# Side test by columns, picked sums right behind the search, the 400-column first count on VectorE, and the last norm batch by batch

## What is computed

```
# attention: 16 heads, 16 memory keys in front of 512 causal ones
dots = where(causal, neg, mix_heads(q @ k.T * scale, pre_proj))
vk   = top_k(dots, 64)[0][..., -1:]          # the 64th largest score of a row
attn = softmax(where(dots < vk, neg, dots))  # only scores >= vk are kept
x    = x + (mix_heads(attn, post_proj) @ v) @ Wo + bo
# mixture of experts: a shared layer and the two best of 8 experts
scores = sigmoid(layernorm(x) @ router_w.T)
gates  = scores * one_hot(top_k(scores, 2)).sum()
x = x + shared(layernorm(x)) + sum_e(expert_e(layernorm(x)) * gates_e)
```

## Time and profile before

| | us |
|---|---|
| median of 3 runs | 1032.5 (1032.15 to 1034.19) |
| the profiled execution | 1035.09 |
| its span, first to last instruction | 1033.4 |
| mean granted clock of PE | 0.951 of full |
| PE / VectorE / ScalarE / GpSimd busy | 909.2 / 849.7 / 747.8 / 468.6 |

### The profile page before, as it was taken

One profiled execution on the slowest core, in us unless ns is written; L12 is line 12 of the kernel. 1 busy time (PEld: TensorE's weight loads), 2 busy tenths in 40 slices (PEclk: granted clock), 3 DMA queues, 4 the chain that ended last, 5 costly groups with the idle time before them and its releaser, 6 DMA issues.

```text
span 1033.4 us, 16125 instructions
## 1 busy us (share of the span) xinstructions
PE 909.2 (88%) x4151; PEld 579.8 (56%) x4151; DVE 849.7 (82%) x2863; ACT 747.8 (72%) x1946; POOL 468.6 (45%) x1109
## 2 busy tenths in 40 slices
PE   8857767999999999999999999788997878999998
PEld 4524434666666666666666666566665655433342
DVE  5687984999999999999999999899999972355443
ACT  6423236899999999999999999789998865221221
POOL 2000013667676676676767767546665650000000
PEclk9867988899999999999999999899999988899999
DMA  5955410000000000000000000000000000000000
GB/s 155 161 115 92 82 10 1 2 2 1 2 2 2 2 1 2 2 1 2 2 2 2 2 2 2 1 2 2 1 2 1 2 1 1 1 10 1 10 11 10
DMA packets 15005, 18.13 MB, mean 18 GB/s; under 512 B 2656, under 2 KB 12192, under 8 KB 14240
## 3 DMA queue, kind: packets, MB, share of 16 engines
q1 hardware_dynamic: 14880, 16.84, 7.8%
HBM read 11.07 MB, written 5.77 MB: 16 GB/s over the span
## 4 chain that ended last, share of the span: by engine, by line
DVE 49%; PE 29%; issue 10%; ACT 7%; POOL 2%; DVEq 2%; POOLq 1%; DMA 0%; ACTq 0%
DVE Ex L1042 11%; DVE top L993 7%; DVE mixed L987 6%; DVE Sx L956 4%; DVE unread L974 3%; PE bH L455 3%; DVE yk L1065 3%; PE bA L560 2%; PE bBC L560 2%; DVE away L981 2%; PE bFGI L441 2%; PE bFGI L579 2%; PE bBC L561 2%; PE bH L579 2%; PE bFGI L561 2%
## 5 line engine op out<-in xcount | busy, mean ns | idle before, releaser
L1251 POOL TENSOR_TENSOR mixed<-Sx,nthr 128x528 f32<-128x528 f32 (+3 forms) x256 | 186.0, 759 | 11.5 <-issue 11.5
L441 PEld LDWEIGHTS bFGI<-spread,Ex 128*128 128x128 f32 x1280 | 154.4, 198 | 62.1 <-POOL spread L1270 60.1
L455 PE MATMUL bH<-turned 128*128 128x512 f32 (+3 forms) x512 | 153.2, 442 | 38.9 <-ACT turned L714 38.6
L441 PE MATMUL bFGI<-spread,Ex 128*128 128x128 f32 x1280 | 163.7, 285 | 20.3 <-POOL spread L1270 20.3
L687 ACT ACTIVATE unread<-Sx,nthr 128x144 bf16<-128x144 f32 (+3 forms) x256 | 143.9, 563 | 21.8 <-POOL nthr L1232 18.1
L455 PEld LDWEIGHTS bH<-turned 128*128 128x128 f32 x512 | 92.0, 189 | 100.0 <-issue 79.7
L695 ACT ACTIVATE unread<-mixed,least 128x528 bf16<-128x528 f32 (+3 forms) x256 | 143.4, 566 | 0.0
L1042 DVE SCALAR_TENSOR_TENSOR Ex<-mixed,yk,Ex 128x144 f32<-128x144 f32 (+3 forms) x256 | 139.6, 598 | 1.7 <-ACT Ex L706 1.0
L706 ACT ACTIVATE Ex<-Sx,nmax 128x144 f32<-128x144 f32 (+3 forms) x256 | 125.5, 563 | 0.0
L993 DVE MAX8 top<-mixed 128x8 f32<-128x528 f32 (+3 forms) x256 | 110.7, 493 | 0.0
L1270 POOL TENSOR_TENSOR spread<-ident,rinv 128x512 f32<-128x512 f32 x64 | 66.6, 1041 | 84.3 <-DVE rinv L1045 84.3
(11 more groups left out here) (322 smaller groups left out, 1802.7 us busy)
## 6 DMA issues: line engine op xcount, KB each, us to landing
heads_store<-per_head SPq DMA_DIRECT2D x2, 1152.0 KB, 5.0
mixed<-heads_store SPq DMA_DIRECT2D x16, 144.0 KB, 10.9
mixed_store<-mixed SPq DMA_DIRECT2D x2, 1152.0 KB, 4.1
per_head<-mixed_store SPq DMA_DIRECT2D x16, 144.0 KB, 6.0
xr<-in_xT SPq DMA_DIRECT2D x4, 256.0 KB, 3.7
w_s<-in_w12T SPq DMA_DIRECT2D x1, 1024.0 KB, 14.1
outT<-xc SPq DMA_DIRECT2D x4, 256.0 KB, 2.0
wq_s<-in_WqT SPq DMA_DIRECT2D x1, 512.0 KB, 3.8
```

What stands on the lines that cost most here:

```text
L441: last = mm(bFGI[:, k * P:k * P + P], Ex[g % 2][:, t, a:a + P], spread[:, t, :], start=True, stop=True)
L455: last = mm(bH[:, jt * P:T], u[:, jt, :], PT[:, at:at + n], start=h + jt == 0, stop=False)
L1251: Gp.tensor_tensor(y[ph][t], Sx[ph][:, t, 0:NT[t]], nthr[ph][1][:, t:t + 1].broadcast_to((P, NT[t])), ALU.add).then_inc(sem("y_ready"), 1)
```

## The change

1. **The first count of the 400-column tile goes from ScalarE to VectorE** in all steps: `range(2)` becomes `range(3)` in VectorE's `tally`, `range(2, TT)` becomes `range(3, TT)` in `first_tally`, and the host's table of steering numbers treats tile 2 as a count instead of a sum of signs.
2. **Side test by columns**: `away` is four `tensor_scalar` instructions of one column each instead of one `tensor_tensor` of four columns.
3. **Sums of picked values directly behind the search**: `pick_tops` and `add_tops` follow `nearest`, and `last_kept` comes after `fetch(0)`, ahead of fetches 1 and 2. `pick_tops` waits for `pick_ready` by itself.
4. **Last norm by batch**: means, variances and scaling of batches 0 and 1 stand in steps 62 and 63, those of batch 2 around the last `values`, those of batch 3 between the first units. Roots go to ScalarE in groups (`roots`), the diagonals to GpSimd. The first unit starts before the last batch's attention sum. The router runs in units 2 and 4.
5. **Unit order**: the shared units of batches 0 and 1, then their expert units, then the same for 2 and 3. `route` and `weigh_experts` stand behind units 5, 6, 18 and 20.

Diff, cut to its core (`up`, `route` and the other helpers keep their arithmetic; only banks and waits differ):

```diff
+ORDER = [(b, u) for pair in ((0, 1), (2, 3)) for us in (range(SH), range(SH, UNITS)) for b in pair for u in us]
+
+
...
+        diag4 = [x[:, :, :].rearrange("p t n -> p (t n)")[:, TT * NE * NE + k * T:TT * NE * NE + k * T + T] for x in Sx for k in range(2)]
...
+        ln4_bank = [bBC[:, 0:512], bBC[:, 512:1024], bA[:, :], bF]
+        half_bank = [(bBC[:, 0:512], bI), (bA[:, :], bBC[:, 512:1024])]
...
+            def mean4(b):
+                pe.wait_ge(sem("sum_taken"), b + 1)
+                mm(ln4_bank[b], mean_w[:, :], xr[:, b, :], start=True, stop=True).then_inc(sem("ln_mean"), 1)
...
+            def var4(b):
+                pe.wait_ge(sem("ln_sq"), 3 * B + b + 1)
...
+            def wide4(b):
+                pe.wait_ge(sem("ln_diag"), 3 * B + b + 1)
+                mm(ln4_bank[b], ones_w[:, :], diag4[b], start=True, stop=True).then_inc(sem("ln_wide"), 1)
...
+            def route(b):
+                pe.wait_ge(sem("ln_out"), 3 * B + b + 1)
+                for t in range(TT):
+                    last = mm(bE[:, (TT * b + t) * NE:(TT * b + t + 1) * NE], xn[:, b, t * P:t * P + P], rw_s[:, :], start=True, stop=True)
+                last.then_inc(sem("route_done"), 1)
...
+            def turn_gates(b):
+                pe.wait_ge(sem("gates_ready"), b + 1)
+                if b % 2:
+                    pe.wait_ge(sem("gT_copied"), b)
+                for t in range(TT):
+                    last = mm(octo[4][0:3 * NE, t * P:t * P + P], gates[:, TT * b + t, :], ident_h[:, :], start=True, stop=True)
+                last.then_inc(sem("gT_done"), 1)
...
+            def up(i):
+                b, u = unit(i)
+                pe.wait_ge(sem("ln_out"), 3 * B + max(b + 1, min(2 * i + 1, 3)))
...
+            def down4(i):
+                b, u = unit(i)
+                if u == 0 and b >= 2:
+                    pe.wait_ge(sem("out_ready"), b - 1)
+                pe.wait_ge(sem("mo_ready"), i + 1)
...
             for g in range(-2, HEADS + 1):
                 if g == 1:
                     pe.wait_ge(sem("ln_out"), 3 * B)
-                if g == HEADS:
-                    pe.wait_ge(sem("fetched"), TT * HEADS)
-                    pe.wait_ge(sem("hits_read"), HEADS)
-                    means(3, range(B - 1))
                 if 0 <= g - 1:
                     turn_weights(g - 1)
+                if g == HEADS:
+                    wide4(0)
+                    wide4(1)
+                    pe.wait_ge(sem("hits_read"), HEADS)
+                    mean4(2)
...
+                if g == HEADS:
+                    var4(2)
+                    up(0)
...
-            pe.wait_ge(sem("score_ready"), 1)
-            up(0)
+                if g == HEADS - 2:
+                    pe.wait_ge(sem("fetched"), TT * HEADS)
+                    mean4(0)
+                    mean4(1)
+                if g == HEADS - 1:
+                    var4(0)
+                    var4(1)
+            wide4(2)
+            mean4(3)
             for i in range(B * UNITS):
                 b, u = unit(i)
+                if b % 2 and u == SH - 1:
+                    turn_gates(b)
                 if i + 1 < B * UNITS:
                     up(i + 1)
-                if u == 0 and b >= 2:
-                    pe.wait_ge(sem("out_ready"), b - 1)
-                pe.wait_ge(sem("mo_ready"), i + 1)
-                w = s3_s[:, u, :] if u < SH else w3_s[:, u - SH, :]
-                last = mm(octo[6 + b % 2], w, mo_h[:, i % 2, :], start=u == 0, stop=u == UNITS - 1)
-                last.then_inc(sem("mo_down"), 1)
+                if b % 2 and u == SH - 2:
+                    turn_gates(b - 1)
+                down4(i)
+                if i == 0:
+                    var4(3)
+                if i == 2:
+                    wide4(3)
+                    for b in range(B - 1):
+                        route(b)
+                if i == 4:
+                    route(B - 1)
...
-                for t in range(2, TT):
+                for t in range(3, TT):
...
+            def roots(first, end):
+
+                act.wait_ge(sem("ln_inv"), 3 * B + end)
+                rows = rstd[:, TT * first:TT * end]
+                nc.scalar.activation(rows, rows, ACT.Sqrt).then_inc(sem("ln_root"), 1)
...
-                if g >= HEADS:
-                    squares(3, range(B - 1))
                 if 0 <= g - 1:
                     turned_copy(g - 1)
+                if g == HEADS:
+                    squares(3, (2,))
...
-            squares(3, (B - 1,))
-            diagonals(3)
-            act.wait_ge(sem("route_done"), 1)
...
+                if g == HEADS - 2:
+                    squares(3, (0, 1))
+                if g == HEADS - 1:
+                    roots(0, 2)
+
+            roots(2, 3)
...
+                if b % 2 and u == SH - 1:
+                    for k in (b - 1, b):
+                        act.wait_ge(sem("gT_done"), k + 1)
+                        nc.scalar.activation(gT[k % 2][:, :], octo[4][0:3 * NE, :], cp).then_inc(sem("gT_copied"), 1)
+                if i == 0:
+                    squares(3, (B - 1,))
+                if i == 1:
+                    roots(B - 1, B)
+                if i == 5:
+                    act.wait_ge(sem("route_done"), B)
...
-                for t in range(2):
+                for t in range(3):
...
-                V.tensor_tensor(away[:, :], over[g % 2][:, :], steer_s[:, 5, :], ALU.add).then_inc(sem("away_ready"), 1)
+                for t in (3, 2, 1, 0):
+                    last = V.tensor_scalar(away[:, t:t + 1], over[g % 2][:, t:t + 1], steer_s[:, 5, t:t + 1], None, ALU.add)
+                last.then_inc(sem("away_ready"), 1)
...
 
+                dve.wait_ge(sem("pick_ready"), g + 1)
                 dve.wait_ge(sem("topped"), 2 * g + 2)
                 V.tensor_tensor(picked_top[:, :, :], pick[:, :, 0:WIN], top[:, :, :], ALU.mult).then_inc(sem("top_picked"), 1)
...
                     if g > H and g % H == 1:
                         take_sum(g // H - 1)
+                    pick_tops(g)
                     read_hits(g)
+                    add_tops(g)
                 if coming:
                     free_for_fetch(g + 2)
                     fetch(g + 2, (0,))
                 if there:
-                    pick_tops(g)
-                if coming:
-                    fetch(g + 2, (1,))
-                if there:
-                    add_tops(g)
-                if coming:
-                    fetch(g + 2, (2,))
-                if there:
                     last_kept(g)
                 if coming:
+                    fetch(g + 2, (1, 2))
                     measure_first(g + 2)
                     fetch(g + 2, (3,))
                 if there:
@@ -1110,12 +1177,12 @@
...
-            centre(3, range(B - 1))
-            take_sum(B - 1)
...
-            centre(3, (B - 1,))
-            scale(3)
+                if g == HEADS - 2:
+                    centre4(0)
+                    centre4(1)
+                if g == HEADS - 1:
+                    deviation(3, 0, ln4_bank[0])
+                    deviation(3, 1, ln4_bank[1])
...
+                dve.wait_ge(sem("mo_down"), last_unit(b) + 1)
...
+            normed(3, 0, ln4_bank[0])
+            normed(3, 1, ln4_bank[1])
+            centre4(2)
+            deviation(3, 2, ln4_bank[2])
+            take_sum(B - 1)
+            normed(3, 2, ln4_bank[2])
+            for i in range(B * UNITS):
+                weigh_half(i)
                 if i == 0:
-                    route(0)
-                elif u == UNITS // 2 and b < B - 1:
-                    route(b + 1)
-                if i == 1 or u == UNITS // 2 + 1 and b < B - 1:
-                    dve.drain()
-                    weigh_experts(0 if i == 1 else b + 1)
+                    centre4(3)
+                if i == 1:
+                    deviation(3, 3, ln4_bank[3])
+                if i == 3:
+                    normed(3, 3, ln4_bank[3])
+                if i == 5:
+                    dve.wait_ge(sem("score_ready"), 1)
+                for b in range(B):
+                    if i and i - 1 == last_unit(b):
+                        add_out(b)
+                for b, at in enumerate((5, 6, 18, 20)):
+                    if i == at:
+                        route(b)
+                        dve.drain()
+                        weigh_experts(b)
...
+            for b in range(B):
+                pool.wait_ge(sem("ln_root"), max(b, 1) + 1)
+                Gp.tensor_tensor(diag4[b].rearrange("p (t n) -> p t n", t=TT), ident[:, :].unsqueeze(1).broadcast_to((P, TT, P)),
```

More of the change, by code:

```diff
@@ L508, in _ @@
             mean3(2)
+            def mean4(b):
[4 more added lines that the diff above has]
+                for t in range(TT):
+                    last = mm(ln4_bank[b][:, t:t + 1], sq[:, b, t * P:t * P + P], mean_w[:, 0:1], start=True, stop=True)
+                last.then_inc(sem("ln_var"), 1)
@@ L509, in _ @@
+            def down4(i):
[3 more added lines that the diff above has]
```

(42 more changed lines are left out.)

34 lines of the change are left out of this document (23 added, 11 removed).

## The result

The changed kernel takes 1054.5 us (median of 4 runs, 1053.96 to 1054.6), the kernel before 1033.4 beside it: over all runs a ratio of 1.018, 95% interval 1.014 to 1.023. Run again later, with 6 runs, it took 1048.0 against 1037.5: 1.011 (1.008 to 1.014). It is slower, by 1 to 2%.

The account below looks back on a forecast made before the run. VectorE was taken to set the step of 10.15 us. Steps plus 27, batch ends minus 4 and norm minus 7 made plus 16, so 1048 us on the median of 1032.5; range 1013 to 1056.

Parts of the forecast that it names:

- Third count: VectorE, early in a step: the 400 columns cost about 0.57 us; ScalarE loses some 0.6, which moves nothing there.
- Side test: VectorE after the counts: four short instructions cost 0.40 us (0.34 to 0.6), so `near` starts at 1.98 after `rinv`.
- Sums behind the search: VectorE from `near` to `yk`: search 2.89 us, then 0.77; `yk` ready at 5.64 in place of 5.99.
- `yk` ends with the first `shift` instruction: `yk` on VectorE still waits for GpSimd's `shift`, to 6.44 us after `rinv`, for 0.80 in place of 0.45.
- `shift` starts at 5.36, and the change frees nothing there: GpSimd's `shift` starts 5.36 us after `rinv`; the change neither touches nor frees what it hangs on.
- Behind `yk`: VectorE from `yk` to the next `rinv`: two fetches add 0.85 us, up to 0.34 comes back; step 10.61.
- Batch ends: Three times VectorE idles 1.63 us for ScalarE's count; 1.3 saved each, minus 4 us in all (0 to 5).
- Norm: Last norm by batch, from `turn_weights(63)` to the last product: minus 7 us (minus 13 to minus 1).
- The move of `yk` gains nothing: VectorE within a step: `yk` issued earlier only waits longer for `shift`, 0.80 us in place of 0.45.
- held and saved: Rival: `near` holds `nthr`, `shift` starts 0.3 us later, `yk` slips in ahead at 0.15; 1017 us, chance 0.28.
- Not held: `near` and `nthr` start side by side; with `near` leading by 0.07 us at most, GpSimd's `nthr` isn't held.
- The norm gives nothing back: Rival at the kernel's end: the gates' stall takes the norm's whole gain; 1055 us, inside the range, no own chance.

Follow-up runs that it names:

- the norm alone: Kernel before with only the last norm by batch, its router products and the new unit order: 1033.4 against 1033.0 us, 0.9985.
- the sum in PSUM: Changed kernel with the sum behind the search written to PSUM, so `yk` has one input in SBUF: 1029.4 against 1033.0 us, 0.9939.
- part 1 alone: Kernel before with only the third count moved to VectorE: 1081.0 us, 1.0433.
- part 3 alone: Kernel before with only products, reads, sum and `yk` moved behind the search, two fetches behind `yk`: 1036.2 against 1036.4 us, 1.0018.
- the three together: Kernel before with third count, side test in four pieces and sums behind the search, old norm and unit order: 1051.4 us, 1.0162.
- the sum in PSUM and the old side test: Changed kernel with that sum written to PSUM and `away` as one instruction again: 1021.6 against 1037.5 us, 0.984.

## Why the prediction came out as it did

The direction and the mechanism at `yk` were right: 1048 forecast, 1054.5 and 1048.0 measured. That the sum came so close is partly luck. The steps cost 7.5 us less than forecast, the batch ends gave back 2.6 less and the norm 5.5 less: 19.5 - 1.4 from the profiles and - 1.5 for the norm alone make 16.6, against a forecast of 16. By its steps:

- *Third count*: 0.57 forecast, 0.55 from start to start (424.80 to 425.35). Right.
- *Side test*: 0.40 forecast, 0.57 measured, inside the 0.34 to 0.6. The step that failed is "a short instruction costs 0.08": the four begin 0.12 apart, and each takes 0.205, not 0.16. `near` started at 2.13, not 1.98. And the one instruction that they replaced took 0.25 there when it was put back, so part 2 makes each step's search 0.3 later for nothing.
- *Sums behind the search*: 0.77 + 2.89 forecast, 3.72 measured from `near` to `yk`.
- *`yk` ends with the first `shift` instruction*: right in every ordinary step, and shown by the sum in PSUM. It takes 0.48, below the 0.7 to 0.9 that I gave as the sign, as it is issued at 5.85, not 5.64, and `shift` is 0.12 earlier.
- *`shift` starts at 5.36, and the change frees nothing there*: this reading failed. I had read it off one step. In 25 of the steps of the kernel before, `moved` waits for ScalarE's first count, meets `near` and is held; `nthr` then comes at 2.32 after `rinv` (433.80) and `shift` at 5.71:

```profile
435.61 0.36 POOL L1230 TENSOR_TENSOR moved<-above,cf 128x4 f32<-128x4 f32 x1 [0.26 <-ACT unread L679]
436.12 0.20 POOL L1232 TENSOR_TENSOR nthr<-moved,cf 128x4 f32<-128x4 f32 x1
...
439.51 1.07 POOL L1251 TENSOR_TENSOR mixed<-Sx,nthr 128x528 f32<-128x528 f32 x1 [0.18 <-issue]
```

  With the third count gone from ScalarE, `moved` starts at 1.52 (425.55, after the `rinv` of 424.03), `nthr` at 1.86 and `shift` at 5.24 in nearly every step:

```profile
425.55 0.20 POOL L1311 TENSOR_TENSOR moved<-above,cf 128x4 f32<-128x4 f32 x1
```

  This is why the step became 10.50 and not 10.61. The 58 steps from 0 to 61 that are no batch ends cost 19.5 together, 0.34 each, and not 27.
- *Behind `yk`*: 0.85 - 0.34 on 3.66 gave 4.17; measured 434.53 - 430.36 = 4.17.
- *Batch ends*: minus 4 forecast. They went from 12.2, 12.4 and 11.5 to 11.6, 11.6 and 11.5: minus 1.4. "Three times VectorE sits idle" was wrong: before, it waited for that count 1.46 and 1.63 at the first two ends, and not at the third. With the change these two waits are 0.38 and 0.39.
- *Norm*: minus 7 (minus 13 to minus 1) forecast; alone it gave 1.5 (minus 4 to plus 1). The stall for the gates and the fewer overlaps were there: PE waits 2.61 for the gates and 0.77 for their copy, and the first expert's two products take 2.08, where such a pair took 1.12 in the earlier trace rows: behind the waits PE runs at half clock (the third number from the right in the last row, 0.50 granted from 923 to 926, after 1.00 from 915 to 919), which I had not priced.

```profile
919.33 0.39 PE L543 MATMUL bE<-ident_h,gates 128*24 128x128 bf16 x4 [2.61 <-DVE gates L1216]
920.49 0.58 PE L556 MATMUL bE<-unread,onehot 24*128 24x512 bf16 x1 [0.77 <-ACT unread L843]
921.00 2.08 PE L559 MATMUL bBC<-xn,w_s 128*128 128x512 f32 x2
```
```profile
923.00:926.00 3.00, 3.00 (x5) 0.88 (x3) 0.56 (x1) 0.60 (x1) 0.00 (x0) 0.50 0.00 0
```

  What I mis-sized is the gain. From `turn_weights(63)` to the last product I had 170.7 (852.7 to 1023.4); the eight profiles with the new norm take 169.6 to 174.5, and the kernel before 176.4, but the four others with the old norm only 172.5 to 173.1. I had taken one execution for the old norm's price, the longest of five.
- *"The move of `yk` gains nothing"* holds for the move by itself (1.0018), but it was not tested against the order that the rest of the change would otherwise have had. There the products would have been late as well, and the move saves 35 us. The parts of this change don't add up: 45 for part 1 alone, nothing that shows for part 3 alone, 18 for the three together.
- *The rivals*: "held and saved" needed `near` some 0.05 ahead of `nthr`. With four pieces it came 0.27 after it, since `near` was later and `nthr` earlier than forecast. "Not held" was right by luck: I allowed a lead of 0.07 and called it not held, but in the changed kernel a lead of 0.09 did hold `cf` (0.47 in place of 0.20). In all thirteen traces, 204 of GpSimd's small instructions (`moved`, `nthr`, `cf`) start up to 0.045 behind the first of `near`, and none is held; of 35 at 0.046 to 0.048, 12 are; and all 453 from 0.049 to 0.30 end 0.55 to 0.56 behind its start, whatever their own start. So a lead of 0.05 decides, between the 0.02 and the 0.25 of the earlier trace rows. By the rule that whoever issues first keeps the pair of ports for its whole instruction (the Trainium skill, SBUF — State Buffer, "Who interferes with whom") the traces agree from a lead of 0.049 on, and not below 0.046. The case itself did occur, in four steps of the kernel with part 1 alone and in some of the kernel with the sum in PSUM and the old side test. "The norm gives nothing back" (1055) was nearly the case.

## What to carry to other kernels

Where two engines hold each other up, write down for each instruction that can be held when it is issued and when the other's long instruction begins and ends, and redo that table for every version: the loss jumps by nearly a whole instruction (0.9 us here) at a crossing of 0.03, and freeing one instruction can just have the next ones held. Look at many steps and not at one: here the other engine's long instruction started at two places by turns. Take the cause away first (one of the two inputs in PSUM), which alone gained nothing here (1.004), then arrange the rest so that long reads of two SBUF tiles start where the other engine stops; only then is work that is moved off a neighbour worth its price. Read single-execution differences of a few us against the spread of several executions.
